# Linear attention in two halves of four head groups, its feed-forward fed by an exchanged projection, with the root norm's factor applied at the end

## The reference, cut to what matters

```python
# stage l3a: x = x + attn(layernorm(x)); h = 16 heads, d = 8, 128 tokens
q = (x @ Wq.T).reshape(b, t, h, d); k = ...; v = ...          # same for k, v
surprise = sigmoid(maximum(x @ Wm1.T + bm1, 0) @ Wm2.T + bm2) # one number per token and head
decay = 1.0 - surprise
def step(state, (qt, kt, vt, dt, gt)):                         # scan over the tokens
    state = state * dt + gt * (kt[..., :, None] * vt[..., None, :])
    return state, einsum('bhd,bhde->bhe', qt, state)
y = ys.reshape(b, t, c) @ Wproj.T
yn = y * rsqrt(mean(y ** 2) + eps)                             # the root norm
mlp = square(maximum(yn @ Wfc.T, 0)) @ Wcp.T                   # 128 -> 512 -> 128
return y + mlp
```

## Time and profile before

| | |
|---|---|
| runs of the kernel before | 555.61 us median (554.93, 555.61, 557.3) |
| the profiled execution | 555.55 us, of it 553.7 us span |
| first matmul of `l3a` behind its layer norm | at 498.43 us |
| first instruction behind the last `Wcp` matmul (L396) | at 522.20 us |
| last product of `l3f` ends | at 551.76 us |
| TensorE, VectorE, ScalarE, GpSimd busy over the span | 87%, 61%, 42%, 12% |

### The profile page before, as it was taken

One profiled execution on the slowest core, in us unless ns is written; L12 is line 12 of the kernel. 1 busy time (PEld: TensorE's weight loads), 2 busy tenths in 40 slices (PEclk: granted clock), 3 DMA queues, 4 the chain that ended last, 5 costly groups with the idle time before them and its releaser, 6 DMA issues.

```text
span 553.7 us, 10384 instructions
## 1 busy us (share of the span) xinstructions
PE 481.9 (87%) x4252; PEld 387.3 (70%) x4252; DVE 339.2 (61%) x807; ACT 233.4 (42%) x464; POOL 66.1 (12%) x129
## 2 busy tenths in 40 slices
PE   8988998999763958899988789779999999999695
PEld 6856885554553857555456679659999999889595
DVE  5565379872358746988225555466777778645433
ACT  7115426778101423166713336165556565501031
POOL 1310123000015021100022005300000000010000
PEclk9989999999995889999999999989999999999999
DMA  7809002900367436500030000000000000055000
GB/s 275 375 21 201 14 2 47 202 1 2 107 256 280 192 106 240 192 1 2 1 115 1 1 2 2 1 0 1 1 1 1 2 0 1 1 226 231 2 1 5
DMA packets 8018, 43.10 MB, mean 78 GB/s; under 512 B 1114, under 2 KB 3738, under 8 KB 5146
## 3 DMA queue, kind: packets, MB, share of 16 engines
q1 hardware_dynamic: 6388, 33.77, 18.5%
q0 software_dynamic: 1584, 8.68, 4.3%
HBM read 35.76 MB, written 0.08 MB: 65 GB/s over the span
## 4 chain that ended last, share of the span: by engine, by line
PE 63%; DVE 18%; DMA 6%; ACT 5%; issue 4%; POOL 3%; SPq 1%; POOLq 0%; DVEq 0%; ACTq 0%
PE banks L269 57%; PE banks L272 6%; DMA p_const<-in_const 3%; DVE peaks L1472 3%; DMA region<-in_tree_f,leaf_no 1%; ACT probs L1541 1%; DMA region<-in_tree_q,leaf_no 1%; POOL mv L364 1%; ACT probs L720 1%; DVE probs L609 1%; DVE xnT L377 1%; DVE xn L358 1%; DVE nmax L608 1%; DVE nmax L605 1%; SPq L295 1%
## 5 line engine op out<-in xcount | busy, mean ns | idle before, releaser
L269 PE MATMUL banks<-identb 128*128 128x128 bf16 x1106 | 78.6, 226 | 18.5 <-DMA region<-in_tree_q,leaf_no 10.1
L269 PEld LDWEIGHTS banks<-identb 128*128 128x128 bf16 x1106 | 70.9, 102 | 24.7 <-DMA region<-in_tree_q,leaf_no 10.5
L1472 DVE TENSOR_REDUCE peaks<-banks 128x1 f32<-128x1024 f32 x64 | 75.4, 1218 | 8.6 <-PE banks L269 7.6
L2385 DVE TENSOR_REDUCE small<-banks 128x1 f32<-128x1024 f32 x32 | 39.1, 1221 | 23.3 <-PE banks L269 23.1
L272 PE MATMUL banks<-p_first,probs 128*128 128x128 f32 x320 | 44.8, 276 | 7.5 <-DVE weights_lo L2395 2.1
L2473 ACT CAST weights_hi<-banks 128x512 fp32r<-128x512 f32 x64 | 35.5, 587 | 31.4 <-PE banks L272 26.9
L2395 DVE TENSOR_TENSOR weights_lo<-banks,weights_hi 128x512 fp32r<-128x512 f32 x64 | 41.6, 683 | 10.6 <-ACT weights_hi L2473 10.6
L272 PEld LDWEIGHTS banks<-p_first,probs 128*128 128x128 f32 x320 | 36.4, 141 | 16.2 <-issue 6.0
L1541 ACT ACTIVATE probs<-banks 128x512 f32<-128x512 f32 x64 | 33.4, 602 | 27.1 <-PE banks L269 26.8
L1541 ACT ACTIVATE probs<-banks,seen 128x512 f32<-128x512 f32 x64 | 38.8, 687 | 12.6 <-PE banks L269 12.6
L2464 ACT ACTIVATE probs<-banks,nmax 128x1024 f32<-128x1024 f32 x32 | 35.6, 1115 | 18.7 <-DVE nmax L2389 18.6
(11 more groups left out here) (461 smaller groups left out, 881.4 us busy)
## 6 DMA issues: line engine op xcount, KB each, us to landing
region<-in_w_l2f SPq DMA_DIRECT2D x1, 4096.0 KB, 13.3
region<-in_w_l3f SPq DMA_DIRECT2D x1, 4096.0 KB, 13.3
region<-in_w_b SPq DMA_DIRECT2D x1, 3076.0 KB, 13.4
values<-in_ctx SPq DMA_DIRECT2D x2, 1024.0 KB, 7.8
region<-in_w_l0f SPq DMA_DIRECT2D x1, 2048.0 KB, 21.6
keys_l1x<-shared SPq DMA_DIRECT2D x8, 256.0 KB, 4.2
keys_l2x<-probsT SPq DMA_DIRECT2D x8, 256.0 KB, 5.1
region<-in_w_l3d SPq DMA_DIRECT2D x1, 2048.0 KB, 17.0
```

What stands on the lines that cost most here:

```text
L269: return nc.tensor.matmul(o, lhsT, rhs, start=start, stop=stop)
L1472: nc.vector.tensor_reduce(peaks[:, h // 4 % 2, i:i + 1], ps[:, 2 * a:2 * a + 2, :], AX.XY, ALU.max, negate=True).then_inc(VM.sem, VM.now(( ...
L2385: return nc.vector.tensor_reduce(small[:, half:half + 1], ps[:, 2 * half:2 * half + 2, :], AX.XY, ALU.max)
```

## The change

The scan's rows are worked through in two halves, `h = 0` and `1`, of four groups (512 columns, one bank) each. TensorE's order becomes k0, z, v0, q0, both halves of the surprise, k1, v1, q1, each with a step of its own. ScalarE takes over `d = 1 - surprise`, in halves (`Identity`, scale -1, bias a column of ones), beside the copies of k and q, now in halves. VectorE runs the product, the second product, the zeros, the scan and the product with q for one half, then for the other. The first four `gather` matmuls are issued when half 0 is ready; `keep(30, 1)` stands between them and the other four, in place of `keep(92, 1)`.

In the feed-forward a second product with the operands exchanged gives the projection transposed (`l3a.pT`), and `Wfc` is applied to it as it is; the projection in its first form follows for the sum of squares and the residual. The turn `l3a.yn`, its copy and GpSimd's power are gone. `Wfc`'s results go to two banks in halves; ScalarE copies each (256 columns), VectorE makes ReLU and square in one `scalar_tensor_tensor` each. The factor, now a reciprocal on VectorE, is applied in the last instruction, which multiplies `Wcp`'s result and adds `xb`.

```diff
-                for j in range(8):
-                    o, b = (j % 4) * P, j // 4
-                    mm(ps[:, b, o:o + P], wide_k[:, j * P:(j + 1) * P], xnT[:, :])
-                    mm(ps[:, 2 + b, o:o + P], wide_v[:, j * P:(j + 1) * P], xnT[:, :])
-                    m = mm(ps[:, 4 + b, o:o + P], wide_q[:, j * P:(j + 1) * P], xnT[:, :])
-                    if j == 1:
-                        pe.wait_ge(V.sem, V.at("l3a.m1"))
-                        mm(ps[0:H, 7, 0:P], at["w_c.m2"][0:32, :], tA[0:32, :]).then_inc(T.sem, T.now("l3a.z"))
-                m.then_inc(T.sem, T.now("l3a.kvq"))
+                def project(h, first, wide, name):
+                    for j in range(4 * h, 4 * h + 4):
+                        m = mm(ps[:, first + h, (j % 4) * P:(j % 4 + 1) * P], wide[:, j * P:(j + 1) * P], xnT[:, :])
+                    m.then_inc(T.sem, T.now((name, h)))
+
+                project(0, 0, wide_k, "l3a.k")
+                pe.wait_ge(V.sem, V.at("l3a.m1"))
+                mm(ps[0:H, 7, 0:P], at["w_c.m2"][0:32, :], tA[0:32, :]).then_inc(T.sem, T.now("l3a.z"))
+                project(0, 2, wide_v, "l3a.v")
+                project(0, 4, wide_q, "l3a.q")
                 pe.wait_ge(V.sem, V.at("l3a.s"))
                 pe.wait_ge(G.sem, G.at("l3a.sel"))
                 for j in range(8):
                     m = mm(ps[:, 6 + j // 4, (j % 4) * P:(j % 4 + 1) * P],
                            probsT[0:H, j // 4, (j % 4) * P:(j % 4 + 1) * P], tC[0:H, :])
-                m.then_inc(T.sem, T.now("l3a.s"))
-                pe.wait_ge(A.sem, A.at("l3a.k"))
-                keep(92, 1)
+                    if j % 4 == 3:
+                        m.then_inc(T.sem, T.now(("l3a.s", j // 4)))
+                project(1, 0, wide_k, "l3a.k")
+                project(1, 2, wide_v, "l3a.v")
+                project(1, 4, wide_q, "l3a.q")
 
                 for j in range(8):
+                    if j == 4:
+                        pe.wait_ge(A.sem, A.at(("l3a.k", 1)))
+                        keep(30, 1)
                     if j % 4 == 0:
                         pe.wait_ge(V.sem, V.at(("l3a.st", j // 4)))
                     m = mm(ps[:, 0, 0:P], at["gather"][:, 112 - 16 * j:240 - 16 * j], st8[:, j * P:(j + 1) * P], j == 0, j == 7)
                 m.then_inc(T.sem, T.now("l3a.y"))
+                keep(4, 1)
                 pe.wait_ge(V.sem, V.at("l3a.y"))
+                mm(ps[:, 5, 0:P], at["w_c.p"], tB[:, :]).then_inc(T.sem, T.now("l3a.pT"))
                 mm(ps[:, 4, 0:P], tB[:, :], at["w_c.p"]).then_inc(T.sem, T.now("l3a.p"))
-                keep(14, 1)
-                turn_tensor(pe, "l3a.yn", tE[:, :], "l3a.yn", 5)
-                pe.wait_ge(V.sem, V.at("l3a.yn.T"))
+                keep(4, 1)
+                pe.wait_ge(V.sem, V.at("l3a.pT"))
                 for c in range(4):
-                    m = mm(ps[:, 6, c * P:(c + 1) * P], at["w_c.fc"][:, c * P:(c + 1) * P], tF[:, :])
-                m.then_inc(T.sem, T.now("l3a.fc"))
-                keep(11, 1)
-                pe.wait_ge(V.sem, V.at("l3a.fc"))
+                    m = mm(ps[:, 6 + c // 2, c % 2 * P:(c % 2 + 1) * P], at["w_c.fc"][:, c * P:(c + 1) * P], tF[:, :])
+                    if c % 2:
+                        m.then_inc(T.sem, T.now(("l3a.fc", c // 2)))
+                keep(8, 1)
                 for c in range(4):
-                    m = mm(ps[:, 7, 0:P], probs[:, 0, c * P:(c + 1) * P], at["w_c.cp"][:, c * P:(c + 1) * P], c == 0, c == 3)
+                    pe.wait_ge(V.sem, V.at(("l3a.fc", c // 2)))
+                    m = mm(ps[:, 3, 0:P], probs[:, 0, c * P:(c + 1) * P], at["w_c.cp"][:, c * P:(c + 1) * P], c == 0, c == 3)
                 m.then_inc(T.sem, T.now("l3a.cp"))
```

VectorE, from the reciprocal of the surprise on (added lines; what they replace is L2603 to L2633):

```diff
+                for h in range(2):
+                    c = slice(h * BANK, (h + 1) * BANK)
+                    dve.wait_ge(A.sem, A.at(("l3a.k", h)))
+                    dve.wait_ge(T.sem, T.at(("l3a.v", h)))
+                    vl(dve, nc.vector.tensor_tensor(ux[:, c], kx[:, c], ps[:, 2 + h, :], ALU.mult))
+                    dve.wait_ge(T.sem, T.at(("l3a.s", h)))
+                    dve.wait_ge(A.sem, A.at(("l3a.d", h)))
+                    nc.vector.tensor_tensor(ux[:, c], ux[:, c], ps[:, 6 + h, :], ALU.mult)
+                    vl(dve, nc.vector.memset(dx[:, c].rearrange("p (j t) -> p j t", t=P)[:, :, 0:1], 0.0))
+                    vl(dve, nc.vector.tensor_tensor_scan(st8[:, c], dx[:, c], ux[:, c], 0.0, ALU.mult, ALU.add))
+                    dve.wait_ge(A.sem, A.at(("l3a.q", h)))
+                    nc.vector.tensor_tensor(st8[:, c], st8[:, c], qx[:, c], ALU.mult).then_inc(V.sem, V.now(("l3a.st", h)))
                 dve.wait_ge(T.sem, T.at("l3a.y"))
                 nc.vector.tensor_copy(tB[:, :], ps[:, 0, 0:P]).then_inc(V.sem, V.now("l3a.y"))
+                dve.wait_ge(T.sem, T.at("l3a.pT"))
+                nc.vector.tensor_copy(tF[:, :], ps[:, 5, 0:P]).then_inc(V.sem, V.now("l3a.pT"))
                 dve.wait_ge(T.sem, T.at("l3a.p"))
                 vl(dve, nc.vector.tensor_copy(tC[:, :], ps[:, 4, 0:P]))
                 vl(dve, nc.vector.tensor_tensor_reduce(tD[:, :], tC[:, :], tC[:, :], 1.0, 0.0, ALU.mult, ALU.add, s[:, 1:2]))
+                for h in range(2):
+                    dve.wait_ge(A.sem, A.at(("l3a.fc", h)))
+                    o = probs[:, 0, (2 * h + 4) * P:(2 * h + 6) * P]
+                    nc.vector.scalar_tensor_tensor(probs[:, 0, 2 * h * P:2 * (h + 1) * P], o, 0.0, o, ALU.max,
+                                                   ALU.mult).then_inc(V.sem, V.now(("l3a.fc", h)))
+                vl(dve, nc.vector.tensor_scalar(mv[:, 2:3], s[:, 1:2], 1.0 / P, float(np.finfo(np.float32).eps), ALU.mult,
+                                                ALU.add))
+                nc.vector.reciprocal(mv[:, 3:4], mv[:, 2:3])
+                vl(dve, nc.vector.tensor_tensor(xb[:, :], tC[:, :], xs[:, x_at[tag], :], ALU.add))
+                dve.wait_ge(T.sem, T.at("l3a.cp"))
+                nc.vector.scalar_tensor_tensor(xs[:, 1 - x_at[tag], :], ps[:, 3, 0:P], mv[:, 3:4], xb[:, :], ALU.mult,
+                                               ALU.add).then_inc(V.sem, V.now("l3a.x"))
```

ScalarE, behind the exp of `z` (`copy_half(dst, name, first, h)` waits for the TensorE step `(name, h)` and copies bank `first + h` to half h of `dst`; these replace L2641 to L2643):

```diff
+                copy_half(kx, "l3a.k", 0, 0)
+                for h in range(2):
+                    act.wait_ge(T.sem, T.at(("l3a.s", h)))
+                    nc.scalar.activation(dx[:, h * BANK:(h + 1) * BANK], ps[:, 6 + h, :], ACT.Identity, bias=one[:, 0:1],
+                                         scale=-1.0).then_inc(A.sem, A.now(("l3a.d", h)))
+                copy_half(qx, "l3a.q", 4, 0)
+                copy_half(kx, "l3a.k", 0, 1)
+                copy_half(qx, "l3a.q", 4, 1)
+                for h in range(2):
+                    act.wait_ge(T.sem, T.at(("l3a.fc", h)))
+                    nc.scalar.copy(probs[:, 0, (2 * h + 4) * P:(2 * h + 6) * P], ps[:, 6 + h, 0:2 * P]).then_inc(
+                        A.sem, A.now(("l3a.fc", h)))
```

More of the change, by code:

```diff
@@ L2514, in l3a @@
             T.plan("l3a.m1")
[L2515 to L2521, removed]
+            V.plan("l3a.m1", "l3a.nb")
+            T.plan(("l3a.k", 0), "l3a.z", ("l3a.v", 0), ("l3a.q", 0), ("l3a.s", 0), ("l3a.s", 1), ("l3a.k", 1),
+                   ("l3a.v", 1), ("l3a.q", 1))
+            A.plan("l3a.z", ("l3a.k", 0), ("l3a.d", 0), ("l3a.d", 1), ("l3a.q", 0), ("l3a.k", 1), ("l3a.q", 1),
+                   ("l3a.fc", 0), ("l3a.fc", 1))
+            V.plan("l3a.s", ("l3a.st", 0), ("l3a.st", 1))
             T.plan("l3a.y")
             V.plan("l3a.y")
[L2524 to L2529, removed]
+            T.plan("l3a.pT", "l3a.p")
+            V.plan("l3a.pT")
+            T.plan(("l3a.fc", 0), ("l3a.fc", 1))
+            V.plan(("l3a.fc", 0), ("l3a.fc", 1))
             T.plan("l3a.cp")
@@ L2536, in l3a @@
             wide_k, wide_v, wide_q = keysT[:, 0:n8], keysT[:, n8:], shared[:, n8:]
-            G.plan("l3a.rstd", "l3a.sel", "l3a.rs")
+            G.plan("l3a.rstd", "l3a.sel")
             @on("pe")
@@ L2622, in _ @@
                 vl(dve, nc.vector.tensor_tensor_reduce(tD[:, :], tC[:, :], tC[:, :], 1.0, 0.0, ALU.mult, ALU.add, s[:, 1:2]))
[L2623 to L2627, removed]
-                turn_vector(dve, "l3a.yn", tF, 5)
-                dve.wait_ge(T.sem, T.at("l3a.fc"))
-                vl(dve, nc.vector.tensor_scalar(probs[:, 0, BANK:2 * BANK], ps[:, 6, :], 0.0, None, ALU.max))
-                nc.vector.tensor_tensor(probs[:, 0, 0:BANK], probs[:, 0, BANK:2 * BANK], probs[:, 0, BANK:2 * BANK],
-                                        ALU.mult).then_inc(V.sem, V.now("l3a.fc"))
-                end_vector(dve, tag, ps[:, 7, 0:P], xb[:, :], "l3a.cp")
+                for h in range(2):
[10 more added lines that the diff above has]
+                                               ALU.add).then_inc(V.sem, V.now("l3a.x"))
             @on("act")
@@ L2640, in _, with copy_half @@
                                      scale=-1.0).then_inc(A.sem, A.now("l3a.z"))
```

(10 more changed lines are left out.)

## The result

The changed kernel took 549.68 us (median of 549.32, 549.68 and 550.43) against 555.61 us, a ratio of 0.9883 with a 95% interval of 0.9857 to 0.9909. That is faster by 1.2%. The forecast was 548.9 us in a range of 547.8 to 551.4. Its direction and its range held; of the 6.8 us forecast, 5.9 came.

What follows compares the result with a forecast made beforehand. The stage was taken as a line of dependent steps across engines. Gains of 3.7 us up to `y` and 3.1 in the feed-forward sum to 6.8, taking the profiled 555.55 to 548.8, median 548.9; range 547.8 to 551.4 us.

Steps and rivals of the forecast that it cites:

- The line of dependent steps: Whole stage: engines hand over without waiting for transfers, so each microsecond off the line shortens the program by one.
- ScalarE's d on the line: Attention, half 0: d0 by `Identity` takes 0.687 us while VectorE waits; part of the 3.7 us gain up to `y`.
- Scan of 512: Attention, VectorE: a half's scan takes 1.22 us, bounds 1.15 to 1.45, against 2.30 for the whole.
- The feed-forward: From `y` seen to the stage's last instruction: 4.15 + 0.06 us instead of 7.29, gain 3.1 us.
- Half 1 under cover: Attention: k1 ready 0.6 to 0.7 us before VectorE needs it; `keep(30)` ends 0.5 us before delaying anything.
- table load: Rival: `Identity` makes ScalarE change tables, 1.28 us a load, two on the line; gain 4.2, time 551.4; chance 0.04.
- ScalarE did not become the bound: Rival: slower ScalarE copies make d0 0.33 later and k1 0.4 late; gain 6.1, time 549.6; chance 0.05.
- Both parts gave their gain: Rival: attention halves or exchanged projection gives nothing through an unseen wait; gain 3.1 to 3.7, 552 to 552.5; chance 0.04.
- the longest idle stretch of TensorE in the new order is 0.6 us: Argument against the slower-clock rival: TensorE idles at most 0.6 us, against 0.90 before ahead of `Wcp`, where the clock stayed.
- The short fall: Rival: fewer keeps let TensorE's clock fall for some 4 us of work, giving 551 to 553 us; chance 0.03.
- a granted clock of 1.00 up to 542: Sign named for a correct forecast: TensorE's clock stays at its upper level until 542 us.
- 567 us for a clock at half throughout: Slower rival: next stage's 16.36 us of chain matmuls take twice that at 1.2 GHz; chance 0.03 for slower.

Runs made afterwards that it cites:

- the kernel with the turn: Changed kernel with the projection made once and turned by TensorE instead of a second product with exchanged operands; 550.72 us, ratio 0.9906.
- the feed-forward alone: Kernel before with only the new feed-forward, its attention left as before; 553.37 us, ratio 0.9952.
- d on VectorE: Changed kernel with d = 1 - surprise worked out in halves by VectorE instead of ScalarE; 550.53 us, ratio 0.9908.
- the hidden layer whole: Changed kernel with the hidden layer as before: one bank, ReLU and square as two 512-column VectorE instructions, no ScalarE copy; 550.05 us, ratio 0.9894.
- 38 keeps: Changed kernel with 38 keep matmuls instead of 16 ahead of the next stage's turn; 549.02 us, ratio 0.9892; with d as `Copy` too, 548.89 us.

## Why the prediction was right, and where a term was off

- *The line of dependent steps.* Right. What was taken off the line in this stage came out of the span. The exp of `z` was forecast 1.85 us behind the stage's start and came at 1.85.
- *ScalarE's d on the line.* 0.687 was forecast, 0.69 measured. What I undersized is the hand-over to VectorE: I gave it 0.01 us, it took 0.13 (502.86 + 0.69 to 503.68). With the surprise's matmuls 0.08 and their hand-over to ScalarE 0.04 later than forecast, and 0.04 less from product to scan, the first scan starts at 6.47 us instead of 6.27 and `y` comes at 13.00 instead of 12.80. Gain 3.5, not 3.7. VectorE's wait between the two products of half 0 was 1.76 us instead of 1.4.
- *Scan of 512.* 1.22 forecast, 1.23 and 1.22 measured.
- *The feed-forward.* 4.15 us forecast, 4.20 measured; two copies of 256 columns in 0.82, two ReLUs in 0.80, the last instruction 0.35, whose extra 0.06 shows in the next stage (29.29 against 29.21). Two misses nearly cancel, which is luck: a ReLU with square took 0.42 us, not 0.48, but the hand-over from ScalarE's first copy was again 0.11 (512.90 + 0.37 to 513.38) where I had 0.03 at most. The experiments split the 3.07 us: exchange 0.71, halves 1.02, and the remaining 1.34, by subtraction, is the deferred factor with what it takes off the line. Read from the timelines instead, the factor is worth 1.48: the kernel before takes 2.19 us from the copy of the projection (515.80) to that of the turn (517.99), and the kernel with the turn 0.71. The halves are then worth 0.88; the 0.14 us between the two ways are those of the hidden layer above.
- *Half 1 under cover.* k1 had 0.85 us to spare, not 0.6, and the keeps ended 0.49 us early, as forecast.
- *The rivals.* No table load stands in the stage. ScalarE did not become the bound; giving VectorE the work back made it slower by 0.67. Both parts gave their gain.
- *What was off.* The step that failed is the sentence that the longest idle stretch of TensorE in the new order is 0.6 us. I had looked only inside the stage, and I measured it against 0.90 us in the kernel before, which had longer ones too, 1.07 and 1.23. Behind the stage, between 16 keeps and the next turn, TensorE idles for 1.38 us (1.23 before; the last instruction now starts 0.28 us behind the keeps instead of 0.20, and is 0.06 longer). The short fall, to which I gave 0.03 and 551 to 553 us, happened in the profiled execution, at a cost of 0.7 us (29.29 to 30.02), not 2 to 4, and the sign that I had named, a granted clock of 1.00 up to 542, failed. It explains why the stages gained 5.8 us in that profile and 6.5 in the one without a fall. Whether it has a part in the median is open: the other runs have no profile, and the start of the stage alone scatters by more.
- *Slips in the working.* 567 us for a clock at half throughout doesn't follow from its terms: 548.9 + 16.4 is 565.3. ScalarE's copy of q is not the only work beside the line of the kernel before; the surprise's matmuls (504.83, 2.05 us) run beside the copy of k. The range of 547.8 to 551.4 is narrower above than the bounds and the spread of the runs together (550.2 + 1.7). None of the three moves the forecast.

The gain without a fall on either side is 52.98 - 46.49 = 6.5 us, against 6.8 forecast. The old feed-forward has a stretch of 1.08 us ahead of the turn, which the change removes; the stretch of 1.23 us behind the stage stays and grows to 1.38. Behind the 1.23 no fall came in three profiles, so that the change made this risk larger is only argued.

Left open: what decides whether a fall follows a stretch of 1.08 or 1.38 us, and whether that one stretch is its cause. Behind the 1.08 it came in two profiles of four, behind 1.36 to 1.38 in two of six (the changed kernel twice, the feed-forward alone, d on VectorE, the turn, the hidden layer whole), never in three with 38 keeps, nor behind 1.13 us (hidden layer whole) or 1.21 us (d on VectorE) in one profile each. In the kernel with the turn it began some 2.2 us behind the end of the stretch, when TensorE had been busy without a pause since 519. To let VectorE's second product run beside ScalarE's d, both reading the same PSUM bank, was not tried.

## What to carry to other kernels

Rebuild the line of dependent steps from the stage's own rows, hand-overs included; halves of 512 or even 256 columns pay as long as the other engine's work is really beside them, and it is worth asking which half of a move pays (here only half 1 of d). When a stage gets shorter, look also at the idle stretches at its borders, where filler work was counted out for the old order: here 22 more fillers cost nothing, and the fall of 0.7 us came in none of the three profiles that had them, which may still be luck; leaving all fillers out cost 2.4 to 3.2 us in the one profile of it. Where whole runs scatter by more than the effect, compare stages inside the profiles.

## What the runs showed of the hardware that I had not expected

TensorE's clock fell to 1.2 GHz 0.85 to 2.2 us behind idle stretches as short as 1.08 us, with work on both sides of them, and it did so in one of two profiles of the same kernel. Each such fall cost 0.7 to 0.85 us on the line.

The same code ahead of the stage let it start anywhere from 495.58 to 500.27 us in 14 profiles: 4.7 us of scatter that no edit here touches, more than either half of the change is worth.
